# First half's experts as one block inside the second half's attention of a Flamingo-style two-layer kernel

## What is computed

```python
x = x + tanh(g_xattn[0]) * _L0_xattn_ref(_layernorm(x), ctx_1024, ...)   # 16 heads of 64
x = x + tanh(g_ffn[0])   * _L0_ffn_ref(_layernorm(x), ...)               # 8 experts, hidden 256, relu
x = x + tanh(g_xattn[1]) * _L1_xattn_ref(_layernorm(x), ctx_1024, ...)   # 1 head of 128
x = x + tanh(g_ffn[1])   * _L1_ffn_ref(_layernorm(x), ...)               # shared expert + 8 experts, hidden 512, silu
```

## Time and profile before

| | us |
|---|---|
| three runs | 324.93, 323.88, 320.55 |
| median | 323.88 |
| the profiled execution | 319.63 |
| its span, first to last instruction | 317.9 |
| PE, DVE, ACT, POOL busy in the span | 268.3, 192.8, 154.9, 93.9 |
| mean granted TensorE clock | 0.946 |

### The profile page before, as it was taken

How to read it: one execution, slowest core, us unless ns; L and a number is a source line. 1 busy time by engine, 2 the same in 40 slices (tenths; PEclk the granted TensorE clock), 3 DMA queues, 4 the chain that set the end, 5 groups by cost and what they waited for, 6 DMA issues and landing times.

```text
span 317.9 us, 6233 instructions
## 1 busy us (share of the span) xinstructions
PE 268.3 (84%) x2073; PEld 231.7 (73%) x2073; DVE 192.8 (61%) x614; ACT 154.9 (49%) x374; POOL 93.9 (30%) x140
## 2 busy tenths in 40 slices
PE   1998986989989988899999999586798975799960
PEld 0577855778868777798988997574788964799950
DVE  2789836688899975347777487865445730122232
ACT  3582466778876666213342441602559620356420
POOL 1265012578854341021002010550100720035053
PEclk9999999899999999989999999787799995999995
DMA  7799885000000000100000000066800148943132
GB/s 194 250 314 243 217 176 118 1 4 5 26 2 2 3 0 2 36 2 0 0 2 0 2 1 0 20 214 163 276 19 2 41 152 278 278 113 87 34 92 66
DMA packets 30847, 27.31 MB, mean 86 GB/s; under 512 B 2705, under 2 KB 24329, under 8 KB 30816
## 3 DMA queue, kind: packets, MB, share of 16 engines
q1 hardware_dynamic: 29408, 24.45, 26.7%
q0 software_dynamic: 1408, 2.46, 3.1%
HBM read 19.17 MB, written 7.73 MB: 85 GB/s over the span
## 4 chain that ended last, share of the span: by engine, by line
PE 52%; DVE 19%; issue 12%; POOL 8%; DMA 4%; SPq 3%; ACT 2%; POOLq 0%; DVEq 0%; ACTq 0%
PE bank L1386 12%; PE bank L1361 6%; PE bank L1373 5%; PE bank L1194 4%; PE bank L1196 4%; PE bank L1195 3%; PE bank L1179 3%; POOL p_sb L625 3%; DVE xhat_sb L895 3%; DVE sum_sb L832 3%; PE bank L1139 2%; DMA ctx_tok_sb<-in_ctx 2%; PE bank L1150 2%; POOL w_q_sb L664 2%; DVE x_sb L1119 2%
## 5 line engine op out<-in xcount | busy, mean ns | idle before, releaser
L779 ACT ACTIVATE p_sb<-bank,bias_t_sb 128x128 f32<-128x128 f32 x120 | 33.8, 374 | 32.5 <-PE bank L1361 32.4
L625 POOL TENSOR_TENSOR p_sb<-p_sb,recip_sb 128x480 f32<-128x480 f32 x32 | 31.6, 988 | 52.1 <-DVE recip_sb L835 52.1
L768 ACT ACTIVATE hT_sb<-bank,cols_sb 128x512 f32<-128x512 f32 x40 | 27.1, 690 | 40.5 <-PE bank L1196 40.3
L1373 PE MATMUL bank<-we_sb,p_sb 128*128 x240 | 32.3, 280 | 3.5 <-issue 3.5
L673 POOL TENSOR_TENSOR rstd_sb<-veps_sb,minus_half_sb 128x4 f32<-128x4 f32 (+1 forms) x11 | 10.6, 966 | 83.1 <-DVE veps_sb L887 82.9
L1386 PEld LDWEIGHTS bank<-w_sb,hT_sb 128*128 128x128 f32 x256 | 32.0, 200 | 2.1 <-issue 1.3
L1373 PEld LDWEIGHTS bank<-we_sb,p_sb 128*128 128x128 f32 x240 | 29.6, 195 | 4.9 <-issue 4.8
L1386 PE MATMUL bank<-w_sb,hT_sb 128*128 128x128 f32 x256 | 32.8, 284 | 0.0
L1119 DVE SCALAR_TENSOR_TENSOR x_sb<-bank,wts_sb,x_sb 128x128 f32<-128x128 f32 x64 | 18.0, 344 | 19.3 <-PE bank L1386 19.2
L652 POOL DMA_INDIRECT xs_hbm<-xhat_sb,slots_sb x16 | 15.7, 983 | 40.9 <-DVE slots_sb L809 36.7
L1150 PE MATMUL bank<-ident_sb,p_sb 128*120 128x128 f32 x128 | 20.2, 285 | 7.7 <-POOL p_sb L625 7.4
(11 more groups left out here) (221 smaller groups left out, 590.6 us busy)
## 6 DMA issues: line engine op xcount, KB each, us to landing
xs_hbm<-col_rows_sb SPq DMA_DIRECT2D x2, 2048.0 KB, 19.6
tile_w_sb<-in_L_ffn_We SPq DMA_DIRECT2D x15, 256.0 KB, 3.6
w_sb<-in_L_ffn_We SPq DMA_DIRECT2D x8, 256.0 KB, 4.0
w_after_sb<-in_L_ffn_We SPq DMA_DIRECT2D x7, 256.0 KB, 3.7
w_kv_sb<-in_L_xattn_w_kv SPq DMA_DIRECT2D x2, 512.0 KB, 6.6
w_sb<-in_L_ffn_w SPq DMA_DIRECT2D x1, 1024.0 KB, 10.9
xs_sb<-xs_hbm SPq DMA_DIRECT2D x15, 64.0 KB, 2.8
w_kv_sb<-xs_hbm SPq DMA_DIRECT2D x15, 64.0 KB, 2.9
```

The costliest lines, as they stand in the source:

```text
L625: nc.gpsimd.tensor_tensor(p0[j % 4], p0[j % 4], recip0[:, j % 2, :].unsqueeze(2) .broadcast_to([128, HG, SK]), ALU.mult).then_inc(probs_re ...
L768: nc.scalar.activation(hT[:, u % 2, c, :], ps(item)[:, :], ACT.Relu if n == 1 else ACT.Silu, bias=cols[:, col:col + 1]).then_inc(read(item ...
L779: last = nc.scalar.activation(hT_t[:, u % RING, c, :], ps(item)[:, 128 * c:128 * (c + 1)], ACT.Silu, bias=bias_t[:, p, c, j:j + 1])
L1373: last = nc.tensor.matmul(dst[:, 0:C], hT_t[:, slot, c, :], we2[:, bass.ds(e, 1), c, :].rearrange("p a h -> p (a h)"), start=(c == 0), sto ...
```

## The change

The list is written anew from attend 18 on; nothing that is computed changes.

1. After attend 27 all eight units of the first half stand as one block (`pause`), with `hot`, `weights`, `wT` and `b2` between them. `k1`, `xT`, `v1`, `logits` and `top` of the first half move ahead of it, among attends 24 to 27.
2. Among attends 28 to 37 stands the first half's second attention, up to `xhat` of stage 3.
3. Then come `xT` to `top` of stage 3, the shared unit `first` and the scatter of the first half, then the eight units of the second half, then the first half's tiles with all of the second half's second attention and router between them.
4. `second` moves from the gathers at the end to the second half's scatter, between the two halves' tiles.
5. `qT`, `kT` and `v0` are laid out by halves. `hT`, `q1T`, `k1T`, `v1`, `p1`, `pT1`, `r1T` and `we1` take the memory of the first half's, which is free once the first half's attention has ended. SP loads `we1` by then.
6. SP stores the first half's results before it loads the second half's tiles, and reads its registers in two parts.

```diff
-    units = expert_units(1, 0) + expert_units(1, 1) + expert_units(3, 0) + expert_units(3, 1)
+    units = expert_units(1, 0) + expert_units(3, 0) + expert_units(1, 1) + expert_units(3, 1)
...
+    first_done = HB * GROUPS - 1 + LY
+    half, quarter = HB, HB // 2
+    beside = {first_done - 4: [("stats", 1, (0, quarter))], first_done - 3: [("xhat", 1, (0, quarter))],
+              first_done + 1: [("stats", 1, (quarter, half))], first_done + 2: [("xhat", 1, (quarter, half)), ("k1", 0)],
+              first_done + 3: [("xT", 1, 0), ("v1", 0)], first_done + 4: [("logits", 1, 0)],
+              first_done + 5: [("top", 1, 0)]}
+    pause = first_done + 5
+    units_in_pause = [[], [], [("hot", 1, 0), ("weights", 1, 0)], [], [("wT", 1, 0)], [], [("b2", 1, 0)]]
+    chain = [[("stats", 2, 0)], [("xhat", 2, 0)], [("xT", 2, 0)], [("q1", 0)], [("s1", 0)], [],
+             [("pT1", 0)], [("o1", 0), ("stats", 3, 0)], [], [("xhat", 3, 0)]]
+    beside.update({pause + 1 + k: items for k, items in enumerate(chain)})
+    beside[pause + 1].insert(0, ("down", *units[E - 1]))
+    beside[pause + 4].append(("split", "we1", 0))
+    beside[pause + 6].insert(0, ("stats", 1, (half, half + quarter)))
+    beside[pause + 7].insert(0, ("xhat", 1, (half, half + quarter)))
+
     for i in range(len(late_queries), STEPS + LY):
         schedule.append(("attend", i))
         if 4 <= i < 4 + 2 * E and i % 2 == 0:
             schedule.append(("split", "w1", (i - 4) // 2))
-        if i in (STEPS, STEPS + 2, STEPS + 4):
-            add_units([tail.pop(0)], [])
...
+        schedule.extend(beside.get(i, []))
+        if i == pause:
+            add_units(expert_units(1, 0), units_in_pause)
+
+
+    schedule += [("stats", 1, (half + quarter, B)), ("consts",), ("xT", 3, 0), ("xhat", 1, (half + quarter, B)),
+                 ("xbias", 3, 0), ("r1", 0), ("up", *first, 0), ("xT", 1, 1), ("logits", 3, 0), ("up", *first, 1),
+                 ("logits", 1, 1), ("top", 3, 0), ("up", *first, 2), ("up", *first, 3), ("hot", 3, 0), ("rank", 0),
+                 *scatters[0], ("top", 1, 1), ("hot", 1, 1), ("weights", 1, 1)]
+    add_units(expert_units(1, 1), [[("wT", 1, 1)], [("tiles", 0)], [("weights", 3, 0), ("b2", 1, 1)], [("k1", 1)],
+                                   [("bias", 0), ("wT", 3, 0)], [("v1", 1)], [("b2", 3, 0), ("yslots", 0)]])
+    schedule.append(("down", *units[unit_at[second] - 1]))
+    tile_items(0, {0: [("stats", 2, 1)], 3: [("xhat", 2, 1)], 5: [("xT", 2, 1)], 7: [("q1", 1)], 9: [("s1", 1)],
+                   14: [("pT1", 1)], 16: [("o1", 1), ("stats", 3, 1)], 20: [("xhat", 3, 1)], 22: [("xT", 3, 1)],
+                   23: [("xbias", 3, 1)], 24: [("r1", 1)], 27: [("logits", 3, 1)], 29: [("top", 3, 1)]})
+    schedule += [("up", *second, 0), ("hot", 3, 1), ("rank", 1), ("up", *second, 1), *scatters[1],
+                 ("up", *second, 2), ("up", *second, 3), ("tiles", 1), ("weights", 3, 1), ("down", *second),
+                 ("bias", 1), ("wT", 3, 1), ("b2", 3, 1), ("yslots", 1)]
+    tile_items(1, {14: [("gather", 0)]})
+    schedule += [("gather", 1), ("comb", 0), ("comb", 1)]
...
+            wait_full(sp, ("s0", HB * GROUPS - 1))
+            wait_full(sp, ("o0", HB * GROUPS - 1))
+            load(we1[:, 0, :], t["L1_ffn_Ws1"], "we1")
...
-                sp.reg_load(e_regs, tile_e[0:1, p, :])
-                sp.reg_load(page_regs, page_of[0:1, p, :])
+                sp.reg_load(e_regs[0:5], tile_e[0:1, p, 0:5])
                 load_w1(p, range(0, 5))
+                sp.reg_load(page_regs[0:TG], page_of[0:1, p, 0:TG])
                 sp.wait_ge(scattered[p], 16 * 2 * HB)
...
                 load_xs(p, 0)
+                sp.reg_load(e_regs[5:], tile_e[0:1, p, 5:])
+                sp.reg_load(page_regs[TG:], page_of[0:1, p, TG:])
...
             load_tiles(0)
-            wait_read(sp, ("down", 1, 1, E - 1))
+            store_ys(0)
             load_tiles(1)
-            store_ys(0)
             store_ys(1)
```

More of the change, by code:

```diff
@@ L57, in expert_units, with tile_items @@
         return [(n, p, e) for e in range(E)] if n == 1 else [(n, p, E)]
[L59 to L70, removed]
+    def tile_items(p, between, lag=2):
+        schedule.append(("gT", p, 0))
+        for j in range(TILES + lag):
+            if j < TILES:
                 if j % TG == TG - 2 and j // TG + 1 < TGROUPS:
@@ L123, in flamingo_kernel @@
         schedule += [("q0", c, 1) for c in chunks]
[L124 to L131, removed]
+    first, second = expert_units(3, 0)[0], expert_units(3, 1)[0]
+    scatters = {p: [("scatter", p, i) for i in range(HB)] for p in range(2)}
+    first_done = HB * GROUPS - 1 + LY
[13 more added lines that the diff above has]
+    beside[pause + 7].insert(0, ("xhat", 1, (half, half + quarter)))
     for i in range(len(late_queries), STEPS + LY):
@@ L135, in flamingo_kernel @@
             schedule.append(("split", "w1", (i - 4) // 2))
[L136 to L139, removed]
-        if i in (STEPS, STEPS + 2, STEPS + 4):
-            add_units([tail.pop(0)], [])
-    n_tail = 3 - len(tail)
-    def with_gaps(items, after):
-        return [part for item in items for part in ([[item], []] if item[0] in after else [[item]])]
-    rest = add_units(expert_units(1, 0)[n_tail:], one_by_one(
-        [("stats", 1, 1), ("xhat", 1, 1), ("k1", 0), ("xT", 1, 1), ("logits", 1, 1), ("top", 1, 1), ("v1", 0),
-         ("hot", 1, 1), ("weights", 1, 1), ("k1", 1), ("v1", 1), ("wT", 1, 1), ("b2", 1, 1)]))
@@ L159, in flamingo_kernel @@
-    chain[0] = [("consts",)] + chain[0]
-    rest = add_units(expert_units(1, 1), chain)
-    first, second = expert_units(3, 0)[0], expert_units(3, 1)[0]
-    schedule.append(("down", *units[unit_at[first] - 1]))
-    for items in rest:
-        schedule.extend(items)
-    scatters = {p: [("scatter", p, i) for i in range(HB)] for p in range(2)}
-    schedule += [("up", *first, 0), ("up", *first, 1), ("up", *first, 2), ("hot", 3, 0), ("rank", 0),
-                 ("up", *first, 3), ("scatter", 0, 0), ("stats", 2, 1), *scatters[0][1:], ("tiles", 0),
-                 ("xhat", 2, 1), ("weights", 3, 0), ("down", *first), ("xT", 2, 1), ("bias", 0), ("q1", 1),
-                 ("wT", 3, 0), ("s1", 1), ("b2", 3, 0), ("yslots", 0), ("pT1", 1), ("o1", 1)]
@@ L171, in flamingo_kernel @@
-    between = {0: [("stats", 3, 1)], 4: [("xhat", 3, 1)], 6: [("xT", 3, 1)], 7: [("xbias", 3, 1)], 8: [("r1", 1)],
-               11: [("logits", 3, 1)], 13: [("top", 3, 1)], 17: [("hot", 3, 1), ("rank", 1), *scatters[1]],
-               19: [("tiles", 1)], 21: [("weights", 3, 1)], 24: [("bias", 1), ("wT", 3, 1)],
-               27: [("b2", 3, 1), ("yslots", 1)]}
-    between = {divmod(k, 2): items for k, items in between.items()}
-    between[TILES + 6, 0] = [("gather", 0)]
-    tile_items(between)
@@ L706, in _ @@
                     wait_full(act, item)
[L707 removed]
+                    nc.scalar.mul(qT[p][:, c, :], ps(item)[:, :], SCALE0).then_inc(read(item), 1)
                 elif kind == "attend":
```

76 lines of the change are left out of this document (33 added, 43 removed).

## The result

| | before | after |
|---|---|---|
| median, us | 322.22 (318.84 to 324.93, 4 runs) | 340.03 (339.53 to 343.46, 4 runs) |
| ratio, 95% interval | | 1.0659 (1.053 to 1.0788) |
| profiled execution, us (span) | 319.63 (317.9) | 339.53 (337.8) |
| TensorE busy, us | 268.3 | 268.8 |

The change makes the kernel 6.6% slower. The profiled span grew by 19.9 us where the prediction had 7.4; the medians of four runs lie 17.8 us apart. All medians here count every execution, while the ratios leave out those in a slower state of the chip, which show a lower clock. First the shares and the clock line of the changed kernel's page, which answer to the earlier trace rows.

What follows compares the result with a forecast made beforehand. TensorE's own work plus its holes was taken as the bound: 94.15 + 15.65 + 25.8 + 44.3 + 33.5 + 40.0 + 20.1 + 34.6 + 17.2 = 325.3 us against 317.9; median forecast 331.3, range 319 to 339.

Steps and rivals of the forecast that it cites:

- the drain: Attends 28 to 38 and the way to the second half's experts: 44.3 us, with TensorE idle 9 to 13 us.
- Part 5: First half's tiles: 40.0 us, against 36.3 before, ending at 253.4.
- ScalarE's change from Exp to Silu: Router steps: each table change costs 1.28 us; the skill's further 1.38 us of drain was left out.
- part 7: Second half's tiles, from gT to the last dnt: 34.6 us, ending at 308.1.
- make gT of group 1 late by 0 to 2 us: +1: Second half's tiles: SyncE's 21 register reads, at most 4.4 us, delay the second row group's gT; 1 us charged.
- parts 1 and 3: Attends 23 to 27 with four small items, 15.65 us; attends 28 to 38 and the way into the tiles, 44.3 us.
- One sign that I named: First half of the 45 us after the block: VectorE busy at 8 tenths or more.
- the rival with VectorE as the bound: From attend 28 VectorE bounds and TensorE drops to half clock: part 3 takes 52 us, total 339; chance 0.12.
- parts 2 and 4: First half's block of eight experts, 25.8 us; second half's experts, 33.5 us; each includes 0.5 us for late weights or scraps.
- part 6: Second half's scatter, last dnt to gT: 20.1 us, bounds 18.5 and 22, with a 10.8 us hole.
- The scatters' landing: Second half's scatter: landing estimated at 2.7 us after the last issue ends, like the row loads' 2.84.
- Nothing is gained by the block itself: First half's eight experts as a block: 25.8 us, work neither cheaper nor dearer than before.

Runs made afterwards that it cites:

- a_early2: Changed kernel with SyncE's register reads put ahead of the wait for the scatters and TensorE's ahead of gT, second run: 335.07 us, ratio 1.0369.
- a_banks: Changed kernel with small PSUM fills among the attends in score banks free at that step, not all in bank 6: 337.79 us, ratio 1.0495.
- b_block: Kernel before with the new buffer layout and five of the first half's eight experts as a block after attend 27: 336.62 us, ratio 1.0388.
- a_nol1: Changed kernel with the first half's second attention left out (statistics, xhat, xT, q1, s1, pT1, o1): 329.61 us, ratio 1.0253.
- second bank rule: Changed kernel with spare banks 0 and 1 in steps 1 and 2 of each four, 5 and 7 otherwise: 347.29 us, ratio 1.0674, on the chip with stalls.
- early reads: SyncE's and TensorE's register reads moved earlier: 315.14 and 314.51 us against the kernel before; 352.25 and 335.07 us in the changed kernel.
- a_regs: Changed kernel with SyncE's registers read whole, right ahead of the weight tiles: 340.77 us, ratio 1.0549.
- a_same: Changed kernel unchanged, run again in another set: 342.77 us, ratio 1.0645.
- a_all: Changed kernel with four mends: second bank rule, SyncE's and TensorE's earlier register reads, and a later first gather: 330.40 us, ratio 1.0214.

## Why the prediction was wrong in size

**Right.** The sign, and where it comes from: the first hole of the earlier trace rows (195.8 to 222.8, 8.2 us of idle time) is gone, the drain takes more than that, and the tail stays 17.2 us and is empty. Part 5 was 39.97 for 40, though its terms were not tried one by one, and the block was busy for 25.9 us where I named 25 to 26. The drain's idle time, 13.0 us, is at the top of the 9 to 13 that I named. Of ScalarE's change from Exp to Silu I took 1.28 us and nothing more, and the changed kernel's rows agree:

```profile
264.69 1.28 ACT L751 ACT_TABLE_LOAD   x1 [0.67 <-PE bank L1180]
...
265.99 2.42 ACT L751 ACTIVATE hT_sb<-bank,cols_sb 128x512 f32<-128x512 f32 x4
```

The activation starts 0.02 us after the load's end. The 1.38 us of drain that the Trainium skill adds ("ScalarE: Activation LUTs", section "What ACT_TABLE_LOAD costs") is not seen after the load here either.

The nine differences in the table of parts sum to the 12.5 us by which the span grew more than I had forecast. They are taken one by one.

**Wrong: part 7, 4.5 us.** The step that failed is "make gT of group 1 late by 0 to 2 us: +1". The reads on SP took 3.5 us and were covered by nothing, the group was 2.46 us late, PE's own read cost 2.64 instead of 1.75, and PE ran its first tiles at 0.62 of its clock. Over my figures the wait for the rows is 1.5 us and the read 0.9; the other 2.1 were no term of mine, and the clock is the nearest cause. a_early2 undoes all of it and PE's read, which I had kept: 32.8 us.

**Wrong: parts 1 and 3, 5.7 us.** I sized waits by what each item needs (its input) and left out where its result goes. With all small items and y0 in bank 6, an item also waits until VectorE has read the one before: 1.41 and 1.25 us in part 1, and 4.8 in part 3 (3.1, 1.3 and 0.4, some 0.8 of the first being xhat's). a_banks shows that a part of it can be had back. Part 3 had 11.3 us of waits and 1.5 of clock in the sum. Measured were 13.0 of waits, of which those that I named are some 8, and 34.5 of busy time against 31.5 at full clock: 3.0. After the wait of 3.11 us the granted clock was 0.50 from 152 to 158 us. One sign that I named failed: VectorE was busy 17.0 of the drain's first 23.7 us, 7 tenths and not 8, so the rival with VectorE as the bound is not borne out either, though its 339 us is near the result.

**Wrong: parts 2 and 4, 4.1 us.** The block has 1.6 us of holes where I gave 0.5, one of them (0.9) again bank 6, read late after b2. Part 4 ran at 0.95 of the clock; in a_banks, with the clock at 1.00, it takes 34.8, so 1.1 us of its 2.4 are the clock's and 1.3 are work and scraps that I sized too low. I had let the lower clock cost something in the drain only. Here PE waited 2.67 us at the end of the drain and 1.01 before 193.8, and from 196 to 198 us it was busy without a hole at a granted clock of 0.50.

**Wrong the other way: part 6, 2.2 us.** The scatters' landing was sized by row loads (2.7 us). SP started its row loads 1.5 us after the last scatter's issue had ended (276.47 to 277.97), and the first tile started 3.6 us after that where I had 4.6. The hole was 8.0 us in place of 10 to 11. Without this error the sum would have missed by 14.7 us.

**What was not priced at all** is how much the old order hid: I took the block as neutral ("Nothing is gained by the block itself") and charged the drain to the chain that came into it. b_block has no such chain there and still loses 13.9 us. a_nol1 says the chain adds 10.4 to the drain. The two can't be added up: they are more than the whole loss, and no run has the drain without both.

Open stay the second bank rule by itself, what part of b_block's loss is in the tiles, the share of SP and of PE in the gain of the early reads, and what VectorE waited for on the one chip.

## What to carry to other kernels

Dense work is worth most where the busiest engine would otherwise wait; gathering it into one block takes its cover away, and the price here was the idle time at its old place plus the clock that this cost. When small items share one result buffer with a loop, each waits for the reader of the one before, so price both what an item needs and whose reading frees its buffer. Look in the issue queue for register reads between two transfers: moving them into a wait that is there anyway, SyncE's and TensorE's together, was worth 7.7 us in one kernel and 7.6 in the other. Moved only as far as in front of other loads of the same chain (a_regs), they showed no gain.

## What the runs showed of the hardware

- The gap in which SP reads 21 registers from a tile, between the first rows and the next weights, is 3.5 us (0.2 with the reads moved, a_same and a_early2), and PE's gap for 15 registers is 1.75 to 2.64 us.
- Indirect DMAs leave POOL one per 1.27 us (1.03 or 0.96 us of issue, 0.30 between), and SP's wait for the last had ended 1.5 us after its issue.
- The granted clock fell by half (from 2.4 to 1.2 GHz) after waits of PE (0.50 from 281.55 to 286 us, after the hole of 5.68 us), not at the same places in each run: the changed kernel's drain had 0.93 in one profile, and a_all's 0.85 with less idle time in it (10.0 us).
- One chip of the three that these sets ran on showed stalls of 4 to 17 us on VectorE and ScalarE while weights and rows were being loaded, in all four kernels profiled there. The kernel before lost 2.1 to 3.1 us there against the other sets, the changed kernel with the early reads 17.2 against its second run. A verdict across chips would have been wrong by more than the effect: only a_same beside a_early2 gave it.
